# Conv, pooled attention, ALiBi attention and a mixture of experts in one kernel: a norm's root behind the masks, statistics and third parts over two steps, and the first score group ahead of the last down product

## The reference

```python
x = x + conv_and_pooled_attention_block(layernorm(x))      # per sequence, with a 128->512->128 gelu MLP
x = x + ffn(layernorm(x))                                  # layer 0, weights Wg, Wu, Wd
x = x + attn_b(layernorm(x))                               # 16 heads of 8, ALiBi, causal
x = x + ffn(layernorm(x))                                  # layer 1, the same weights

def ffn(x):            # 8 experts, all of them added up
    return sum(silu(x @ Wg[e]) * (x @ Wu[e]) @ Wd[e] for e in range(8))     # 128 -> 512 -> 128

def attn_b(x):         # per head h
    q, k, v = split(x @ w_in.T)
    s = q @ k.T / sqrt(8) + slope[h] * (k_pos - q_pos), -inf where k_pos > q_pos
    return softmax(s) @ v, all heads side by side, @ w_out.T
```

## Time and profile before

| | us |
|---|---|
| median of 3 runs | 1829.76 (1827.05 to 1830.11) |
| the profiled execution | 1827.53, of which its span 1825.5 |
| mean granted TensorE clock | 0.981 of full speed |
| TensorE matmul busy | 1707.9 (94%) |
| VectorE busy | 1248.0 (68%) |
| ScalarE busy | 1041.7 (57%) |
| GpSimd busy | 473.7 (26%) |

### The profile page before, as it was taken

The page is one execution under the profiler, slowest core; times in us unless marked ns, Lnnn a source line. Parts: engine busy times, 40 slices in busy tenths (PEclk is TensorE's granted clock), DMA queues, the critical chain, the costliest instruction groups (busy, mean ns, idle before and its releaser), DMA issues.

```text
span 1825.5 us, 28721 instructions
## 1 busy us (share of the span) xinstructions
PE 1707.9 (94%) x10264; PEld 1105.9 (61%) x10264; DVE 1248.0 (68%) x2121; ACT 1041.7 (57%) x1694; POOL 473.7 (26%) x648
## 2 busy tenths in 40 slices
PE   4589999999999999988879999999999999999998
PEld 2257777767776877653334555555555555557877
DVE  3658566856675776767776777777777777746665
ACT  3435655574556555456755666665666566665554
POOL 4712000200020012322112444344434434440000
PEclk8699999999999999999999999999999999999999
DMA  5100000000000023232200010000100000010000
GB/s 173 39 1 1 1 1 1 0 0 0 0 0 0 1 73 110 66 106 75 59 24 25 24 30 7 24 24 6 32 24 25 2 24 2 2 30 1 6 7 6
DMA packets 60521, 47.01 MB, mean 26 GB/s; under 512 B 7647, under 2 KB 58222, under 8 KB 60398
## 3 DMA queue, kind: packets, MB, share of 16 engines
q1 hardware_dynamic: 60224, 45.33, 8.3%
q10 hardware_dynamic: 174, 0.07, 0.0%
HBM read 28.20 MB, written 17.17 MB: 25 GB/s over the span
## 4 chain that ended last, share of the span: by engine, by line
PE 83%; DVE 7%; ACT 4%; issue 3%; POOL 2%; DMA 0%; ACTq 0%; DVEq 0%; POOLq 0%
PE ps L1083 8%; PE ps L1031 7%; PE ps L1084 6%; PE ps L1085 6%; PE ps L912 6%; PE ps L914 5%; PE ps L913 5%; PE ps L1013 4%; PE ps L1115 4%; PE ps L746 4%; PE ps L895 3%; PE ps L1117 3%; PE ps L919 3%; PE ps L1116 3%; PE ps L920 3%
## 5 line engine op out<-in xcount | busy, mean ns | idle before, releaser
L1472 ACT ACTIVATE pr<-ps 128x1024 f32<-128x1024 f32 (+2 forms) x285 | 267.9, 945 | 188.0 <-PE ps L883 118.8
L1803 DVE TENSOR_TENSOR hid<-sg,ps 128x512 f32<-128x512 f32 x256 | 175.1, 684 | 200.2 <-PE ps L914 158.1
L1406 ACT ACTIVATE sg<-ps 128x512 f32<-128x512 f32 x256 | 153.4, 599 | 252.3 <-PE ps L914 250.0
L707 POOL TENSOR_TENSOR h_lo<-hid,h_hi 128x512 fp32r<-128x512 f32 x176 | 225.7, 1282 | 263.5 <-ACT h_hi L1498 259.0
L1793 DVE TENSOR_REDUCE negp<-ps 128x2 f32<-128x1024 f32 (+2 forms) x224 | 254.8, 1146 | 53.7 <-PE ps L883 29.6
L912 PE MATMUL ps<-xn_hi,w_hi 128*128 128x512 f32 x512 | 226.4, 442 | 1.4 <-DVE xn_lo L1649 1.4
L1083 PE MATMUL ps<-xn_hi,w_hi 128*128 128x512 f32 x512 | 223.3, 436 | 0.7 <-DVE hid L1924 0.5
L1924 DVE SCALAR_TENSOR_TENSOR hid<-sg,ps 128x512 f32<-128x512 f32 x176 | 121.0, 688 | 126.2 <-ACT sg L1488 125.5
L914 PE MATMUL ps<-xn_hi,w_lo 128*128 128x512 f32 x512 | 201.9, 394 | 0.0
L1084 PE MATMUL ps<-xn_lo,w_hi 128*128 128x512 f32 x512 | 201.9, 394 | 0.0
L913 PE MATMUL ps<-xn_lo,w_hi 128*128 128x512 f32 x512 | 201.4, 393 | 0.0
(11 more groups left out here) (220 smaller groups left out, 3091.7 us busy)
## 6 DMA issues: line engine op xcount, KB each, us to landing
qs<-qd SPq DMA_DIRECT2D x60, 96.0 KB
ks<-kd SPq DMA_DIRECT2D x60, 96.0 KB
kd<-qkp SPq DMA_DIRECT2D x14, 256.0 KB, 2.9
qd<-qkp SPq DMA_DIRECT2D x7, 384.0 KB, 2.6
x<-in_hidden SPq DMA_DIRECT2D x4, 512.0 KB, 6.8
raw<-in_Wg SPq DMA_DIRECT2D x4, 512.0 KB, 4.5
raw<-in_Wu SPq DMA_DIRECT2D x4, 512.0 KB, 5.5
raw<-in_Wd SPq DMA_DIRECT2D x4, 512.0 KB, 6.6
```

The source lines that it names most:

```text
L707: g.tensor_tensor(h_lo[:, q % 2, :], hid[:, q % 4, :], h_hi[:, q % 2, :].bitcast(F32), ALU.subtract).then_inc(FS[1]["hlo_pool"], 1)
L1472: a.activation(pr_of(n, st)[:].rearrange("p (e a) q -> p e a q", e=2)[:, :, hps[0]:hps[-1] + 1, 0:WIDTH[st]], heads(buf, hps, WIDTH[st]), ...
```

## The change

Six edits:

1. In the last pair VectorE's statistics of a tile to be projected are spread over r = 0 (two bn_stats) and r = 1 (two, then the aggregates), and GpSimd's root moves from r = 0 to r = 2, ahead of that step's `h_lo`. GpSimd's third part of q stays at r = 8, that of k moves to the next r = 0, behind that step's `h_lo`. The norm of tile 7 starts in step 13, not 10.
2. GpSimd makes `h_lo` in steps 45, 46 and 55 too.
3. `scores(0, 0)` and the first maximum job of unit 1 are issued ahead of the last `down` of layer 0. ScalarE's v copy of tile 6 moves behind the last `h_hi` cast; behind it comes the first exponential, then the copy to `yS`, then the second parts of tile 6. VectorE reduces that job ahead of the last addition to `x`.
4. Tile 7's v product moves from turn 10 of unit 0 to turn 7 of unit 1, its second parts from turn 11 to 10.
5. SyncE stores tile 7 during unit 1, behind that unit's first maxima, not during unit 0.
6. In unit 4 GpSimd's root goes behind the second masked block; the normalising moves to k = 14 and 15, the transpose and the split to k = 17, and the wait for them from `maxima_T` to `result_T` at k = 18.

```diff
-REST_BY_POOL = [p for p in EARLY_AT if p not in (45, 46, 55)]
+REST_BY_POOL = EARLY_AT
-PROJECT_LAST = {"stats": 0, "norm": 3, "xT": 4, "q": 6, "k": 8, "v": 10, "second": 11}
+PROJECT_LAST = {"stats": 0, "norm": 3, "xT": 4, "q": 6, "k": 8, "second": 10, "v": NG_S + 7}
 NORM_AT = (10, 16)
+NORM_AT_LAST = 13
+def norm_at(h, last):
+    return NORM_AT_LAST if last else NORM_AT[h]
...
# SyncE, attention_loads
                     load_unit(2)
+                if n == 1:
                     store_qkv(sp, LAST)
...
# GpSimd
             def project_step(t, r):
-                if r == 0:
-                    pool.wait_ge(G["mv"], (t + 1) * SUB)
-                    rstd4(G, t * 2, mvp, lnp)
+                if r == 0 and t:
+                    third_part(t - 1, 1)
                 if r == 8:
-                    for m in range(2):
-                        pool.wait_ge(G["second"], t * 2 + m + 1)
-                        g.tensor_tensor(part(t, m, 2), rest_of_part(t, m), part(t, m, 1),
-                                        ALU.subtract).then_inc(G["third"], 1)
+                    third_part(t, 0)
+            def root_of_projected(t):
+                pool.wait_ge(G["mv"], (t + 1) * SUB)
+                rstd4(G, t * 2, mvp, lnp)
+            def third_part(t, m):
+                pool.wait_ge(G["second"], t * 2 + m + 1)
+                g.tensor_tensor(part(t, m, 2), rest_of_part(t, m), part(t, m, 1),
+                                ALU.subtract).then_inc(G["third"], 1)
...
-                    if p == NORM_AT[0]:
+                    if p == NORM_AT_LAST:
                         norm(TILES - 1)
+                    if p >= PROJECT_FROM and (p - PROJECT_FROM) % PROJECT_STEPS == 2:
+                        root_of_projected((p - PROJECT_FROM) // PROJECT_STEPS)
                     if p in REST_BY_POOL:
...
+                third_part(LAST - 1, 1)
...
                 if n == 0:
-                    project_step(LAST, 0)
-                if n == MIX - 1:
-                    norm_of_tile(0)
+                    root_of_projected(LAST)
                 for st in MASKED:
                     mask_step(n, st)
                     if n == 0 and st == SUB + 1:
-                        project_step(LAST, 8)
+                        third_part(LAST, 0)
+                        third_part(LAST, 1)
+                    if n == MIX - 1 and st == SUB + 1:
+                        norm_of_tile(0)
...
# TensorE (scores and next_max move out of attention(), unchanged)
-                            if c == NORM_AT[h] + 4 and not end:
+                            if c == norm_at(h, last) + 4 and not end:
...
+                            if end and c == CH - 1:
+                                pe.wait_ge(f["silu"], TILES * CH)
+                                pe.wait_ge(T["m_loaded1"], 32)
+                                scores(0, 0)
+                                pe.wait_ge(f["prod"], TILES * CH)
+                                next_max(0, 0)
                             pe.wait_ge(f["hhi"], k + 1)
...
                     if k == PROJECT_LAST["v"]:
-                        pe.wait_ge(G["rest"], LAST * 2 + 2)
+                        pe.wait_ge(T["ctx"], 2)
...
-                        scores(n, k)
+                        if (n, k) != (0, 0):
+                            scores(n, k)
...
-                        if n == 0:
-                            project_last(k)
+                        if n < 2:
+                            project_last(n * NG_S + k)
...
-                            if k == 14:
-                                pe.wait_ge(T["xadd"], b * 2)
-                                input_T(0, 7)
                         if k == 15:
                             if n == 0:
-                                pe.wait_ge(G["vcopy"], TILES)
+                                pe.wait_ge(G["rest"], TILES * 2)
                             elif g == 0:
-                                pe.wait_ge(f["xlo"], 1)
+                                pe.wait_ge(T["xadd"], b * 2)
                             else:
                                 pe.wait_ge(T["ctx"], n * 2)
+                            if n == 1:
+                                pe.wait_ge(G["vcopy"], TILES)
                             maxima_T(n * 2 + 2)
+                        if k == 17 and n == MIX - 1:
+                            pe.wait_ge(T["m_out"], n * 2 + 3)
+                            input_T(0, 7)
                         if k == 18:
                             pe.wait_ge(T["m_out"], n * 2 + 3)
+                            if n == MIX - 1:
+                                pe.wait_ge(f["xlo"], 1)
                             result_T(n, 1)
-                        for job in range(JOBS_TO[k], JOBS_TO[k + 1]):
+                        for job in range(max(JOBS_TO[k], 1 if n == 0 else 0), JOBS_TO[k + 1]):
                             next_max(n, job)
...
# ScalarE
-                            if last and h * CH + c >= PROJECT_FROM:
+                            if last and PROJECT_FROM <= h * CH + c < 2 * CH - 2:
                                 project_step(*divmod(h * CH + c - PROJECT_FROM, PROJECT_STEPS))
...
                 pair(TILES // 2 - 1, True)
+                project_step(LAST - 1, 7)
+                act.wait_ge(G["stored1"], STORED * 2)
+                act.wait_ge(G["stored2"], STORED * 2)
+                exponentials(0, 0, ring(0, SCORE_POS[0]))
                 act.wait_ge(f["y_done"], TILES + 1)
                 a.copy(yS[:], bank(4)).then_inc(f["y_out"], 1)
+                project_step(LAST - 1, 8)
...
-                        if g == 0 and n and k == 14:
-                            input_out(0, 7)
+                        if k == 17 and n == MIX - 1:
+                            input_out(0, 7)
...
# VectorE
-                if r == 0:
-                    dve.wait_ge(FS[0]["xadd"], t + 2)
-                    stats4(t, t * SUB)
+                if r in (0, 1):
+                    if r == 0:
+                        dve.wait_ge(FS[0]["xadd"], t + 2)
+                    for j in (2 * r, 2 * r + 1):
+                        v.bn_stats(stp[:, j, :], xs(t * SUB + j)).then_inc(G["st"], 1)
+                if r == 1:
+                    dve.wait_ge(G["st"], t * SUB + SUB)
+                    v.memset(fence[:], 0.0)
+                    for j in range(SUB):
+                        v.bn_aggr(mvp[:, j, :], stp[:, j, :]).then_inc(G["mv"], 1)
...
                 v.memset(bank(O_BANK), 0.0).then_inc(T["o_zeros"], 1)
+                reduce_job(0, ring(0, JOB_POS[0]), NG_S)
                 dve.wait_ge(f["yT"], TILES + 1)
...
-                            if k in (12, 13):
-                                half_of_norm(0, k - 12)
-                            if k == 14:
+                            if k in (14, 15):
+                                half_of_norm(0, k - 14)
+                            if k == 17:
                                 tile_rest(0, 7)
```

More of the change, by code:

```diff
@@ L904, in maxima_T, with scores, next_max @@
                           start=True, stop=True).then_inc(T["mT"], 1)
+            def scores(n, k):
+                st, hps = TURNS[k]
+                c, j = STEPS[st]
+                w, from_q = WIDTH[st], max(c * NT, j * P)
+                if n >= MIX:
+                    buf = ps[:, S_BANK:S_BANK + 2, :]
+                    pe.wait_ge(T["exp"], n * NG_S + k)
+                    if n == MIX and k == 0:
+                        pe.wait_ge(T["reduced"], (n + 1) * NG_S)
+                else:
+                    buf = ring(n, SCORE_POS[k])
+                    read_to = issued_to(n, SCORE_POS[k] - BUFFERS)
+                    if read_to[0] > 0:
+                        pe.wait_ge(T["exp"], read_to[0])
+                    pe.wait_ge(T["reduced"], read_to[1])
+                for a, hp in enumerate(hps):
+                    dst = [buf[:, e, a * w:(a + 1) * w] for e in range(2)]
+                    for e in range(2):
+                        r = slice(e * HALF, e * HALF + K2)
+                        mm = pe.matmul(dst[e], k_of(n)[r, hp, j * P:(j + 1) * P], q_of(n)[r, hp, from_q:from_q + w],
+                                       start=True, stop=st not in MASKED)
+                    if st in MASKED:
+                        mm = hide_later([d[:, 0:HALF] for d in dst], (2,))
+                mm.then_inc(T["scores"], 1)
+            def next_max(n, k):
+                nxt = (n + 1) % SLOTS
+                if k in (0, JOBS_KC1):
+                    pe.wait_ge(T[f"loaded{nxt}{1 if k == 0 else 0}"], ((n + 1) // SLOTS + 1) * LOADS)
+                if n >= MIX:
+                    pe.wait_ge(T["reduced"], (n + 1) * NG_S + k)
+                    take_max(k, n + 1, ps[:, J_BANK:J_BANK + 2, :])
+                    return
+                read_to = issued_to(n, JOB_POS[k] - BUFFERS)
+                if read_to[0] > 0:
+                    pe.wait_ge(T["exp"], read_to[0])
+                pe.wait_ge(T["reduced"], read_to[1])
```

(40 more changed lines are left out.)

36 lines of the change are left out of this document (6 added, 30 removed).

## The result

The changed kernel takes 1821.03 us (median of 7 runs, 1817.91 to 1822.75), the kernel before, run beside it on the same chip, 1828.22 (7 runs, 1827.05 to 1830.11). The ratio is 0.9958 [0.9947, 0.9970], a gain of 7.7 us with an interval of 5.5 to 9.7.

What follows compares the result with a forecast made beforehand. TensorE, busy 94%, was taken as the bound, so only idle gaps and low-clock stretches could give time. 6.2 (last pair) + 0 - 0.4 + 6.6 (unit 4) = 12.4 off 1827.5; forecast 1815.5 us, range 1808 to 1822.

Steps and rivals of the forecast that it cites:

- The stalls of the last pair: Last pair: TensorE's eight waits ahead of `down`, 6.9 us shown, were worth 8.6 us and would go.
- The root ahead of `h_lo`: Last pair, steps 30, 39, 48, 57: the later root makes TensorE wait 0.3 to 0.8 each, 2.4 us in all.
- due T + 5.4: Last pair: `down` of r = 2 is due two steps after T, but its `h_lo` is seen at T + 5.95.
- only products and reductions: Last pair, three steps whose `h_lo` GpSimd takes over: VectorE's remaining work has a PSUM input, so the sum stays.
- Rival 1: Last pair: stalls only move, the root costs 1.6 each time, gain 2 instead of 6.2; 1819.5 us, chance 0.12.
- The norm at step 13: Last pair: step 13 carries 2.0 us of VectorE work, but a step with only one set of statistics lost nothing.
- The end of layer 0: Layer 0's end: TensorE's 1.9 us wait for the exponential is moved, not removed; net 0, bounds -2.5 and +1.
- v, net 0.4 lost: Units 0 and 1: moving the v product gains at most 0.9 in unit 0 and costs 1.35 in unit 1.
- what would show the forecast wrong: Signs: root's waits above 1 us, unit 4 above 36, or a low stretch in the last pair or unit 1.
- Unit 4, 6.6: Unit 4: waits for mask, normalised tile and split go; 33.6 us with one low stretch, 6.6 gained, bounds 2.0 and 8.5.

Runs made afterwards that it cites:

- root_r1: Changed kernel, but VectorE makes the whole statistics at r = 0 and GpSimd's root stands at r = 1, behind `h_lo`: 1814.72 us.
- v_back: Changed kernel with the last tile's v product back at turn 10 of unit 0, second parts at 11, its store still in unit 1: 1820.27 us.
- y_first: Changed kernel, but ScalarE makes tile 6's second parts behind its v copy, then copies `yS`, then makes the first exponential: 1819.59 us.
- rest_by_vector: Changed kernel, but VectorE instead of GpSimd makes `h_lo` of steps 30, 39, 48 and 57: 1819.29 us.
- root_y_first: Changed kernel with the edits of root_r1 and y_first together: 1811.87 us.
- without_unit4: Changed kernel with unit 4 as in the kernel before: 1825.86 us, ratio to the kernel before 0.9984.
- norm_ahead: root_r1, with VectorE's normalising also put ahead of the job's reduction in steps 30, 39, 48 and 57: 1817.72 us.
- unit4_only: Kernel before with the change of unit 4 alone: 1821.46 us, ratio to the kernel before 0.9961.

## Why the prediction was right, and where it was not

- **The stalls of the last pair, 8.6 us.** Right: root_r1, which loses nothing to the root, gains 7.9 us on the kernel before up to the last `down` but one (5.3 on the changed kernel, which has 2.6). The working of the term was a little high: the rows give 4.15 - 2.69 = 1.46 lost where 1.32 are shown, so 0.14 more for each of eight and 8.0 in all, not 8.6.
- **The root ahead of `h_lo`, 2.4.** The waits were foretold as 0.3 to 0.8 and are 0.6 (four, 2.3 in all). Against root_r1 these steps cost 3.2.
- **The step that failed** is the one that ended at "due T + 5.4" and did not ask what a late `h_lo` lies beside. It priced the root's delay for TensorE alone; VectorE's normalising kept its old 1.1 us in my sum and became 2.8, another 2.5 us of loss. The last pair gave 2.6 up to the last `down` but one instead of 6.2. I had weighed a conflict between GpSimd and VectorE, but only for VectorE instructions with two SBUF inputs and only in the three steps that GpSimd took over ("only products and reductions"). The steps with the root, where the normalising stands, I did not ask about. Rival 1 had nearly the right size (2), for half the right reason.
- **The norm at step 13.** Taken as free ("lost nothing"); against the old place it costs a net 0.4, 1.2 at steps 17 and 19 less 0.8 at steps 10 to 14, the moved transposes in both.
- **The end of layer 0, 0.** The order forecast on ScalarE is the one in the rows, and the wait did move. The last `down` but one comes 3.66 us earlier than in the kernel before (799.99 against 803.65), the scores of turn 2 3.75 (808.15 against 811.90), so 0.1 was gained. What I did not see is that another order on ScalarE gives 1.2 more.
- **v, net 0.4 lost.** 0.73 gained and 1.21 lost by v_back, 0.5: right for v itself. But unit 0 did not get shorter: from turn 2 to its end it takes 31.85 us against 31.78 before, both at a mean clock of 0.84, so something else in it took back what v gave. The wait of 1.64 us for the store is new there; that it is the cause is not shown. That unit 1 would get a low stretch (0.97, from 30.55 against 29.58 in y_first) was named as what would show the forecast wrong, and it happened.
- **Unit 4, 6.6.** 6.8 to 6.9: right, in the rows that went and in size, with some luck in the size. The forecast was 32.7 at full clock and 0.9 for one low stretch; measured were 33.3 and no stretch. With one, as in six of the other kernels with this edit, or with two, as in rest_by_vector and root_y_first, unit 4 takes 34.3 to 35.6.
- **Sum.** 12.4 less 3.6 (last pair), 1.0 (unit 0, where 0.9 was to be gained behind turn 2) and 0.8 (unit 1, 2.2 longer in place of 1.35), and with 0.1 more at the end of layer 0 and 0.2 in unit 4, is 7.3. The table has 7.2, the ratio 7.7. So the time lies in the range because unit 4 came as forecast; of the 5.8 us forecast for everything else the table shows 0.4 and without_unit4 2.9 by its medians.

## What to carry to other kernels

When an instruction on a shared queue comes later, ask not only who waits for it but what it will now run beside: here a root one step too late made two GpSimd subtractions meet VectorE's `tensor_scalar`, and the second loss (2.5 us) was nearly as large as the first (3.2). Price a moved step with a control, since two of my placements started within 0.3 us of GpSimd's subtraction, where 1.1 us of room was needed, and lost most of their gain. And test each part of a bundle alone: one edit of this change carried 6.8 of the 7.2 us that the table shows, and two of the others hid losses that came off by reordering. Before a unit's gain is put down to an edit, set its mean clock beside that of the other kernel.

## What the runs showed of the hardware

- VectorE's 128x128 `tensor_scalar` from SBUF to SBUF takes 340 ns and up to 1402 beside GpSimd's 128x512 subtraction (1.26 to 1.40 us). The one held up ends about 0.1 us behind the subtraction's end, whether the subtraction began first (norm_ahead) or the group of four did (rest_by_vector, where two of 344 ns came through first). Reductions from PSUM are not touched (1.22 to 1.23).
- A stretch at the low level (1.2 GHz) of about 3.5 us (worked out from the mean clock, 0.94 over 29.3 us) costs 0.9 to 1.1 in units 1 to 3 and 1.0 to 1.2 in unit 4; two in unit 4 cost 2.2 (35.53 and 35.57 against 33.32). In unit 0 it cost 0.8 between the changed kernel and root_r1 (35.81 at 0.81, 34.99 at 0.85, the same code in the unit), and 0.3 between the kernel before and unit4_only (36.25 at 0.86, 35.99 at 0.91). They appear in and vanish from units whose own rows are the same, as units 2 and 3 show across the table, so a gain of 1 us in one unit is not told from them by one execution.
- ScalarE's table load of 1.28 us was not made ahead of time: in the changed kernel it began at 801.34, behind 0.56 us of waiting for its activation's scores, in the kernel before behind 1.14 us of it, and in y_first, where the scores were there, straight behind the copy (804.51).
